# Eight-layer linear-attention encoder with a mixture of experts, one core: attention rows are turned by 32x32 blocks on VectorE and a round trip through DRAM, where TensorE turned them, and all engines get a new order

## The reference, cut to what matters

```
q = phi(h @ wq + bq);  k = phi(h @ wk + bk);  v = h @ wv + bv      # phi(t) = elu(t) + 1, 16 heads of 8
kv = einsum('bshd,bshm->bhdm', k, v)
z  = 1.0 / (einsum('bshd,bhd->bsh', q, k.sum(axis=1)) + 1e-6)
att = einsum('bshd,bhdm,bsh->bshm', q, kv, z).reshape(b, s, d)
h = h + att @ wo + bo
h = _ln(h, g1, be1)
y = gelu(h @ w1 + c1, approximate=False) @ w2 + c2                 # 128 -> 512 -> 128
h = _ln(h + y, g2, be2)
```

## Time and profile before

| | |
|---|---|
| median of three runs | 1062.64 us (1062.22 to 1063.05) |
| profiled execution, its own time | 1060.62 us |
| its span, first to last instruction | 1058.9 us |
| TensorE busy | 986.6 us, 93% of the span |
| ScalarE busy | 836.2 us, 79% |
| GpSimd busy | 832.9 us, 79% |
| VectorE busy | 779.3 us, 74% |
| mean granted TensorE clock | 0.980 |

### The profile page before, as it was taken

How to read it: one execution, slowest core, us unless ns; L and a number is a source line. 1 busy time by engine, 2 the same in 40 slices (tenths; PEclk the granted TensorE clock), 3 DMA queues, 4 the chain that set the end, 5 groups by cost and what they waited for, 6 DMA issues and landing times.

```text
span 1058.9 us, 24788 instructions
## 1 busy us (share of the span) xinstructions
PE 986.6 (93%) x7558; PEld 926.6 (88%) x7558; DVE 779.3 (74%) x2681; ACT 836.2 (79%) x1621; POOL 832.9 (79%) x1209
## 2 busy tenths in 40 slices
PE   5899999999999999999999999999998859989994
PEld 4799998999899989999999999999997759889993
DVE  6777777777677777777777777777788888853545
ACT  6888888888888888988888888888887646665573
POOL 5867888888888888888888888877866677677753
PEclk9999999999999999999999999999999978999997
DMA  4101263135314431453154116501302345567363
GB/s 141 51 1 56 69 158 78 56 104 123 80 58 118 126 78 60 124 131 82 61 147 98 56 61 166 98 2 41 121 1 81 96 131 166 177 192 223 96 183 130
DMA packets 101937, 106.41 MB, mean 100 GB/s; under 512 B 8716, under 2 KB 81427, under 8 KB 101680
## 3 DMA queue, kind: packets, MB, share of 16 engines
q1 hardware_dynamic: 95920, 95.32, 33.2%
q0 software_dynamic: 4544, 8.47, 2.3%
q10 hardware_dynamic: 1344, 1.05, 0.3%
HBM read 56.61 MB, written 45.17 MB: 96 GB/s over the span
## 4 chain that ended last, share of the span: by engine, by line
PE 52%; POOL 18%; DVE 10%; issue 9%; ACT 8%; DMA 2%; SPq 1%; POOLq 0%; DVEq 0%; ACTq 0%
PE psum L1962 12%; PE psum L1839 5%; PE psum L1841 5%; PE psum L1840 5%; PE psum L2121 5%; PE psum L2105 4%; ACT s L1052 4%; PE psum L1886 4%; PE psum L1892 4%; POOL rstd L771 4%; PE psum L1874 3%; POOL xt_lo L890 3%; PE psum L1920 3%; POOL res_a L821 2%; POOL res_a L814 2%
## 5 line engine op out<-in xcount | busy, mean ns | idle before, releaser
L1052 ACT ACTIVATE s<-s,shift,rstd 128x128 f32<-128x128 f32 x496 | 204.1, 487 | 45.4 <-POOL shift L773 44.5
L1962 PE MATMUL psum<-this_w,hid 128*128 128x128 f32 x1792 | 214.3, 275 | 0.0
L1962 PEld LDWEIGHTS psum<-this_w,hid 128*128 128x128 f32 x1792 | 206.9, 192 | 0.0
L1031 ACT ACTIVATE hid<-psum,col 128x512 f32<-128x512 f32 x256 | 159.4, 694 | 2.5 <-PE psum L1841 1.7
L771 POOL TENSOR_TENSOR rstd<-var,neg_half 128x4 f32<-128x4 f32 x132 | 144.3, 1093 | 11.0
L1353 DVE TENSOR_TENSOR s<-psum,res_f 128x512 f32<-128x512 f32 x64 | 44.2, 691 | 94.1 <-PE psum L1962 93.9
L1267 DVE BATCH_NORM_STATS2 stat<-s 128x6 f32<-128x128 f32 x512 | 110.2, 276 | 1.1
L1839 PE MATMUL psum<-x_hi,this_w 128*128 128x512 f32 x224 | 95.5, 426 | 1.2 <-DVE x_lo L1339 1.2
L799 POOL TENSOR_TENSOR res_f<-res_f,row 128x512 f32<-128x512 f32 x64 | 92.3, 1442 | 5.0
L2121 PE MATMUL psum<-heads,hid 128*128 x624 | 85.1, 280 | 6.8 <-ACT hid L1185 4.8
L814 POOL TENSOR_TENSOR res_a<-s,row 128x512 f32<-128x512 f32 x60 | 77.4, 1289 | 15.5 <-ACT s L1052 12.1
(11 more groups left out here) (270 smaller groups left out, 2750.6 us busy)
## 6 DMA issues: line engine op xcount, KB each, us to landing
xs<-pad SPq DMA_DIRECT2D x18, 975.0 KB, 8.8
spill<-xrow SPq DMA_DIRECT2D x26, 512.0 KB, 2.6
feature<-spill SPq DMA_DIRECT2D x104, 128.0 KB, 2.9
res_a<-w SPq DMA_DIRECT2D x28, 256.0 KB
xblk<-xs SPq DMA_DIRECT2D x78, 65.0 KB
row<-rows SPq DMA_DIRECT2D x8, 512.0 KB, 5.2
raw_w<-w SPq DMA_DIRECT2D x15, 256.0 KB, 3.9
this_w<-next_w SPq DMA_DIRECT2D x7, 512.0 KB, 3.2
```

The costliest lines, as they stand in the source:

```text
L1031: a.activation(hid[h][:, c, :], ps(3 + h + c), ACT.Gelu, bias=col[:, bass.ds(lw * FF + (C_C1 + c), 1)]).then_inc(hid_done, 1)
L1052: ins = a.activation(dst[:, t, :], src[:, t, :], ACT.Identity, bias=shift[i][:, t:t + 1], scale=rstd[i][:, t:t + 1])
L1962: ins = t_.matmul(ps(down_bank(l, s, h))[:, t * P:(t + 1) * P], hid[h][:, c, t * P:(t + 1) * P], down[:, c, :], start=c == 0, stop=c == FF ...
```

## The change

In the first 30 of the 32 slots (`turned_late`) the attention rows are no longer turned by TensorE. VectorE transposes 32x32 blocks of them (`turn_att`), SyncE writes 512 KB to a DRAM scratch, waits for that, and reads it back in four pieces of 128 KB (`bounce`). `out_proj` takes its operand from there. It now stands at the head of the next slot's program on TensorE, and what depends on it on VectorE (`add_res1`, `moments1`) moves with it. The two PSUM copies on ScalarE go. The up products, the attention products, the down product of half 1 and the biases use other PSUM banks, and the order within a slot is new on TensorE, VectorE, ScalarE and GpSimd. The core of the diff:

```diff
+LATE = (LAYERS - 1) * SLOTS + 2
+def turned_late(l, s):
+    return l * SLOTS + s < LATE
+def up_bank(l, s, h, c):
+    return ((3, 2, 4, 5), (0, 1, 6, 7))[h][c] if turned_late(l, s + 1) else 3 + h + c
+def x1_bank(l, s, h):
+    return 7 if h == 0 or turned_late(l, s + 1) else 0
+def att_bank(l, s, h):
+    return (4, 0)[h] if turned_late(l, s) else 2 * h
...
         def down_bank(l, s, h):
-            return 3 if h == 0 else 0 if l == LAST and s == 3 else 6
+            return 3 if h == 0 else 0 if (l == LAST and s == 3) or turned_late(l, s + 2) else 6
...
+            def bounce(l, s):
+                i = l * SLOTS + s
+                sp.wait_ge(attt_mm, upto(l, s, 1))
+                wait(sp, attt_sb, 16 * QUADRANTS * i)
+                sp.dma_start(att_spill.rearrange("p f c -> p (f c)"), att_blocks).then_inc(att_spilled, 16)
+                sp.wait_ge(att_spilled, 16 * i + 16)
+                wait(sp, wo_mm, upto(l, s - 1, 1))
+                for f in range(QUADRANTS):
+                    sp.dma_start(att_rows[f * BLOCK:(f + 1) * BLOCK].rearrange("p (q c) -> p q c", q=QUADRANTS),
+                                 att_spill[:, f, :].rearrange("(q j) c -> j q c", q=QUADRANTS)).then_inc(attt_sb, 16)
...
             def layer(l, ring):
                 swap_blocks(l, -3)
                 load_raw(l + 1)
+                if l > 0:
+                    set_wo(l)
+                bounce(l, 0)
                 set_w1(l)
                 if l > 0:
                     fill((l - 1) * PIECES * FILL)
...
                 set_w2(l)
                 if l > 0:
                     fill(((l - 1) * PIECES + 1) * FILL)
+                bounce(l, 1)
                 swap_blocks(l, -1)
...
+                if late:
+                    if p2:
+                        inv_std2(l, s - 2, 0)
+                        inv_std2(l, s - 2, 1)
+                    if swapped(l, s - 3):
+                        lo_moved(l, s - 3, 0)
+                    if p2:
+                        scale_resid(l, s - 2, 0)
+                        offset_resid(l, s - 2, 0)
...
+            def turn_att(l, s, h):
+                wait(dve, att_done, upto(l, s, h))
+                wait(dve, att_spilled, 16 * (l * SLOTS + s))
+                d.transpose(att_turned(h), att[h][:, :, :].rearrange("p t (f j) -> p t f j", f=QUADRANTS)).then_inc(attt_mm, 1)
...
+                    mask_kv(l, s, 0)
+                    mask_kv(l, s, 1)
+                    attend(l, s, 0)
+                    turn_att(l, s, 0)
+                    attend(l, s, 1)
+                    turn_att(l, s, 1)
+                    if p1:
+                        lo_x1(l, s - 1, 1)
...
             def ff_down(l, s, h, between=None):
...
-                if h == 1:
+                if h == 1 and turned_late(l, s + 2):
+                    wait(pe, qt_done, upto(l, s + 2, 0))
+                elif h == 1:
...
+                if turned_late(l, s):
+                    if p1:
+                        out_proj(l, s - 1, 0)
+                        out_proj(l, s - 1, 1)
+                    project(l, s, 0, first, last)
+                    project(l, s, 1, first, last)
...
+                    if p2:
+                        ff_down(l, s - 2, 1)
+                    if p1:
+                        flip_x1(l, s - 1, 0)
+                    if s == 2:
+                        bias_products(l + 1)
+                    key_value(l, s, 0)
+                    key_value(l, s, 1)
+                    attention(l, s, 0, first)
+                    attention(l, s, 1, first)
+                    if p1:
+                        flip_x1(l, s - 1, 1)
+                        ff_up(l, s - 1, 0)
+                        ff_up(l, s - 1, 1)
...
+                    if p1:
+                        ff_down(l, s - 1, 0)
```

More of the change, by code:

```diff
@@ L545, in layer @@
                     fill(((l - 1) * PIECES + 2) * FILL)
+                bounce(l, 2)
                 swap_blocks(l, 0)
@@ L548, in layer @@
                     set_qkv(l + 1)
[L549 to L556, removed]
+                else:
+                    set_wo(LAST)
+                    set_w2(LAST)
+                    load_end_rows()
+                bounce(l, 3)
             layer(0, 0)
@@ L930, in slot @@
                     router_constants(s)
-                if p2:
+                if s == 1 and not last:
+                    sum_rows(l + 1, 1 - ring)
+                    wait(pool, rows_summed, l * 8 + 16)
+                if late:
[7 more added lines that the diff above has]
+                        offset_resid(l, s - 2, 0)
+                elif p2:
                     inv_std2(l, s - 2, 1)
@@ L939, in slot @@
                     resid_a(l, s - 2, 1)
-                if s == 1 and not last:
-                    sum_rows(l + 1, 1 - ring)
-                    wait(pool, rows_summed, l * 8 + 16)
-                elif (s == 2 and l + 1 == LAST) or (s == 3 and l + 1 < LAST):
+                if (s == 2 and l + 1 == LAST) or (s == 3 and l + 1 < LAST):
                     hi_w1(l + 1)
@@ L1123, in slot @@
                     split_moved(l, s - 3, 0)
-                if p2:
+                if p2 and not late:
                     norm2(l, s - 2, 0)
@@ L1857, in project @@
                     wait(pe, xt_lo_done, (2 if s == 0 else HALVES) if first and s < 3 else banks_upto(l, s - 3))
-                elif h == 0 and ((s == 3 and not last) or (first and s == 0)):
-                    wait(pe, bias_done, l * 8 + (16 if s == 3 else 8))
-                elif h == 0 and s == 3:
+                elif h == 0 and first and s == 0:
+                    wait(pe, bias_done, l * 8 + 8)
+                elif h == 0 and s == 3 and last:
                     wait(pe, rb_done, 1)
@@ L2029, in slot @@
                     ff_up(l, s - 1, 1)
-                if first and s == 0:
-                    start(4)
-                    start(5)
                 flip_att(l, s, 0)
@@ L2036, in slot @@
                 flip_att(l, s, 1)
-                if s == 2 and not last:
-                    bias_products(l + 1)
                 if s == 2 and last:
```

195 lines of the change are left out of this document (153 added, 42 removed).

## The result

The change makes the kernel slower: **1282.9 us** median of four runs (1278.8 to 1293.6) against 1062.9 for the kernel before beside it, ratio 1.208 (95% interval 1.200 to 1.216). The forecast was 1171, with a range up to 1215: right in direction, half the size. The profiled execution has a span of 1284.9 us against 1058.9, 226 more, where the forecast had 108 more.

A forecast was written before the change was run, and what follows sets the result against it. A loop through ScalarE and GpSimd was to bound the slot at 28.4 us: 28 slots with bias products 802.9 against 707.5, +95; with start, slot 30 and queue +108, hence 1171 us, full range 1122 to 1215.

The forecast's parts named there:

- TensorE bound before, and no wait to be won: Ordinary slot before: TensorE works 24.49 of 24.60 us; removing eight transposes gives at most 0.88 us a slot.
- The first wait: TensorE ahead of the down product of half 1, waiting for `queries` of half 0 to free its bank: 2.75 us a slot.
- The second wait: TensorE ahead of the up product of half 1, waiting for `lo_x1` behind both turns on VectorE: 1.05 us a slot.
- TensorE's round alone: TensorE's work plus two new waits: 27.4 us a slot; as the rival bound, 1143 us, chance 0.18.
- the trip: Attention rows through DRAM to the `wo` operand: 7.5 us from the turn, 0.3 us wait covered by TensorE's 1.0 slack.
- The clock: Rival: idle gaps lower TensorE's clock in the down product, 1.7 us a slot, +48, 1219 us; chance 0.14.
- The loop through ScalarE and GpSimd: From `queries` through late `norm2`, residual steps and `lo_moved` back to `queries`: sets the slot at 28.4 us; chance 0.62.
- At the start: Slot 1 begins with the DRAM transfer uncovered, 7.5 us, partly filled by the first layer's other starts: +5 us.

The follow-up runs named there:

- experiment 1: Kernel before the change, with ScalarE's copies laying the turned attention rows' tokens 8, 4, 2 and 1 elements apart, two layers each: 1087.9 us.
- Experiment 3: Changed kernel with `lo_x1` of half 1 on VectorE ahead of both turns of the attention rows instead of behind them: 1325.7 us, ratio 1.247.

## Why the prediction was half the size

**TensorE bound before, and no wait to be won: right.** The most that the change could give was 0.88 us a slot, and each wait that it added cost more.

**The first wait, 2.75 us: right.** 2.73 in the row, from the cause named; without the bank's reuse the time falls by 53 us.

**The second wait, 1.05: mechanism right, size off.** 1.69 us. The step took the turn at 0.70 us from a row of the same tile size, but not of the same layout. A turn takes 0.46 more, and with the write laid together the wait was 0.9: the two turns cost 0.8, and the other terms of the step were 0.15 too long.

**The failed step: "TensorE's round alone is therefore 23.6 + 2.75 + 1.05 = 27.4".** It came out at 32.5 in the slot shown, so the round was the bound. It kept the `wo` products at their old 1.7 us start to start. They take 3.83, since their operand lies 32 bytes apart (experiment 1): 2.1 us a slot, 62 us in 29 slots, the largest single miss. The change moved the operand to another tile and layout, and I priced the trip there but not the load from it. No rival held this cost, so the range could not reach the time.

**The clock: a rival that came on top.** I gave it 0.14 as a case by itself, and held against it that 2.75 us is shorter than the one wait of 3.10. The waits of 2.73 lowered it too, to 0.68 in the down product shown, 1.7 us: the rival's own price. But it fell behind eighteen of the 28 waits only, and over the slots it is worth 28 us, where the rival had 48. The Trainium skill (TensorE: Matmul & The Clock Gate, "Why this matters for your kernels") warns of idle gaps between bursts of matmuls. These runs agree that such gaps lower the clock, but the gap that it names is longer than 2.73 us, and here the measurement decides.

**The loop through ScalarE and GpSimd, 28.4: not the bound.** None of TensorE's waits in the slots ends with GpSimd. In the slot shown, `lo_moved` of half 1 ends 1.4 us before the products that need it start (664.21 + 1.29 against 666.87):

```profile
664.21 1.29 POOL L954 TENSOR_TENSOR xt_lo<-feature,xt_hi 128x512 fp32r<-128x512 f32 x1
...
666.87 0.39 PE L1991 MATMUL psum<-xt_hi,this_qkv 128*128 128x512 f32 x1
```

The first wait, the down product behind it and the second wait are in the loop as they are in the round, so the clock and the slower turn lengthen both. The `wo` products are in the round alone: their 2.1 us are enough to turn a loop that is 1.0 above the round into one that is 1.1 below it. So the loop's length was about right, and that it set the slot was wrong.

**The trip: covered, and only just, as said.** `wo` waits for its reads in nine slots, 5 us beside slot 0. Experiment 3 shows what it costs when the second wait that covers it goes. At the start the forecast had +5, and it came to +14: the `wo` products of slot 0 start 9.4 us later (42.99 against 33.64), 8.5 of it idle, and the slot from there to those of slot 1, which the forecast had not counted among the longer ones, takes another 4.9 (30.1 against 25.2).

Together: 2.1 + 1.0 + 0.6 for operand, clock (its mean) and turn, and 0.6 for the ends of groups are 4.3 a slot above the round of 27.4, against 1.0 that the loop was to add; 0.4 for the bias products and some 0.3 for the waits ahead of `wo` bring it to 32.4, near the 32.8 measured. The last 0.4 a slot I did not take apart.

## What to carry to other kernels

Where a change takes an operand from another place, read its access pattern as a cost of the reader and of the writer: price them by a row with the same stride, not of the same size. When a round has no slack, waits are not to be summed at full clock: here a wait of 2.7 us in each slot cost another 1.0 on average behind it. And a loop that comes out 1 us longer than the bounding engine's own round decides nothing until each term of that round has a row.

## What was not expected of the hardware

A stationary operand whose elements lie 8 bytes apart is read almost as fast as one that lies together (2.05 against 1.95 us for sixteen products of 128x128), and at 16 or 32 bytes it takes twice as long (3.90 and 3.97). VectorE's transpose of 128x512 in float32 takes 1.16 us when it writes elements 32 bytes apart, and 0.71 when it writes runs of 32. The same idle time of TensorE, 2.73 us, was followed by matmuls at full speed in ten slots and by slower ones in eighteen.
